# Two-layer graph network: where the rows' attention sums of the front stage are computed, and which engine issues the stores of the turned edges

## The reference

```
# layer 0, 8 heads of 64
wh    = (x @ weight).reshape(n, 8, 64)
awh_i = (wh * linear_i).sum(axis=2)      # the rows' attention sums
awh_j = (wh * linear_j).sum(axis=2)
e     = leaky_relu(awh_i[:, None, :] + awh_j[None, :, :], 0.2)
a     = softmax(e + ((1 - adj) * -1e10)[:, :, None], axis=1)
x     = layernorm(x + einsum('ijh,jhf->ihf', a, wh))
# layer 1, 8 heads of 64
adj1  = maximum(adj, eye)
q, k, v = projections of x with Wqs, Wks, Wvs
s     = q @ k.T / 8 + 0.01 * eye - 1e16 * (1 - adj1)
x     = layernorm(x + einsum('hqm,hmk,hko->qo', softmax(s), v, Wo))
```

## Time and profile before

| what | value |
|---|---|
| median of three timed runs | 4205.13 us (4201.45 to 4205.21) |
| the profiled execution: its own time | 4191.47 us |
| its span, first to last instruction | 4189.7 us |
| PE busy | 3770.2 us (90%) |
| DVE busy | 3506.9 us (84%) |
| ACT busy | 3342.6 us (80%) |
| POOL busy | 429.4 us (10%) |
| mean granted TensorE clock | 0.962 |

### The profile page before, as it was taken

The page is one execution under the profiler, slowest core; times in us unless marked ns, Lnnn a source line. Parts: engine busy times, 40 slices in busy tenths (PEclk is TensorE's granted clock), DMA queues, the critical chain, the costliest instruction groups (busy, mean ns, idle before and its releaser), DMA issues. The chain is left out here.

```text
span 4189.7 us, 104540 instructions
## 1 busy us (share of the span) xinstructions
PE 3770.2 (90%) x42880; PEld 2512.5 (60%) x42880; DVE 3506.9 (84%) x6040; ACT 3342.6 (80%) x4233; POOL 429.4 (10%) x634
## 2 busy tenths in 40 slices
PE   7991499999999959959999999999999999999977
PEld 4551499999999924425555555555555555555533
DVE  6657799999999977678888888888888888888734
ACT  3434699999999822239999999999999999999932
POOL 1211000000000000010110201102111021120100
PEclk9995699999999979969999999999999999999989
DMA  9999855555555377773543534435344353453133
GB/s 339 392 307 229 257 185 167 181 188 189 184 192 166 122 206 241 217 188 92 137 119 90 151 90 130 113 98 152 96 123 128 91 141 100 112 138 92 39 113 140
DMA packets 364121, 674.35 MB, mean 161 GB/s; under 512 B 79584, under 2 KB 239408, under 8 KB 326784
## 3 DMA queue, kind: packets, MB, share of 16 engines
q1 hardware_dynamic: 296448, 574.83, 45.9%
q0 software_dynamic: 24064, 84.37, 6.6%
q10 hardware_dynamic: 43136, 8.53, 1.1%
HBM read 524.43 MB, written 143.20 MB: 159 GB/s over the span
## 5 line engine op out<-in xcount | busy, mean ns | idle before, releaser
L1241 DVE CUSTOM_DVE_ANT_0 m_junk<-m_rough,m_rows 128x1024 bf16<-128x1024 f32 x1006 | 1230.8, 1223 | 220.6 <-PE m_rough L1109 207.6
L1187 ACT ACTIVATE m_scores<-m_strip 128x1024 f32<-128x1024 fp8e4 x1024 | 1052.4, 1028 | 121.5 <-DVE m_most L1241 56.8
L1201 ACT ACTIVATE m_whole<-m_scores 128x1024 int32<-128x1024 f32 x1024 | 1037.9, 1014 | 15.8 <-PE m_scores L1142 5.5
L632 PE MATMUL g_acc<-g_vals,g_pos 128*128 128x130 f16 x8192 | 956.6, 218 | 49.3 <-DVE g_neg L587 49.3
L549 ACT ACTIVATE g_step<-g_arow,k_steep 128x512 fp8e4<-128x512 f32 x1536 | 948.4, 707 | 40.7 <-DVE g_pos L580 37.7
L632 PE MATMUL g_acc<-g_vals,g_neg 128*128 128x130 f16 x8192 | 956.1, 221 | 0.0
L1123 PE MATMUL m_acc<-m_v,m_halves 128*128 128x129 f16 (+1 forms) x16384 | 896.8, 208 | 45.4 <-ACT m_got L1164 45.4
L1123 PEld LDWEIGHTS m_acc<-m_v,m_halves 128*128 128x128 f16 x16384 | 750.8, 98 | 280.1 <-issue 185.8
L632 PEld LDWEIGHTS g_acc<-g_vals,g_pos 128*128 128x128 fp8e4 x8192 | 802.1, 98 | 60.2 <-DVE g_neg L587 36.5
L1137 PE MATMUL m_scores<-m_qA,m_kA 128*128 128x512 f16 x2048 | 780.7, 381 | 10.0 <-ACT m_scores L1187 5.4
L632 PEld LDWEIGHTS g_acc<-g_vals,g_neg 128*128 128x128 fp8e4 x8192 | 785.0, 96 | 0.0
(11 more groups left out here) (162 smaller groups left out, 3034.6 us busy)
## 6 DMA issues: line engine op xcount, KB each, us to landing
g_vals<-scr_gat_v SPq DMA_DIRECT2D x128, 1040.0 KB, 5.1
m_v<-scr_v SPq DMA_DIRECT2D x64, 1032.0 KB, 7.7
a_stage<-in_adj SPq DMA_DIRECT2D x64, 1024.0 KB, 9.4
m_kA<-scr_k_hi SPq DMA_DIRECT2D x128, 512.0 KB, 6.2
scr_row_mask<-a_rowm SPq DMA_DIRECT2D x64, 512.0 KB, 8.0
m_rows<-scr_row_mask POOLq DMA_DIRECT2D x64, 512.0 KB, 7.0
m_kB<-scr_k_lo SPq DMA_DIRECT2D x64, 512.0 KB, 5.3
scr_gat_v<-a_early POOLq DMA_DIRECT2D x32, 520.0 KB, 10.6
```

The lines of the kernel that those rows point to most:

```text
L632: mm = pe.matmul(acc[:, b, it, lo:hi], edges[:, n % RING, t, rows], vals[:, b, 4 * j + t, lo:hi], start=j == 0 and t == 0 and lo == 0, sto ...
L1187: nc.scalar.activation(scores[:, n % 2], strip[:, 2 * st:2 * st + 2, :].rearrange("p t i -> p (t i)"), ACT.Copy, bias=-BIG, scale=BIG / ED ...
L1201: nc.scalar.activation(whole[:, st % 2], scores[:, st % 2], ACT.Exp, scale=0.125).then_inc(exped, 1)
L1241: nc.vector.tensor_tensor_reduce(out=junk[:, n % 2], in0=rough_of(m), in1=rows[:, n % TC, n // TC * WIDE:(n // TC + 1) * WIDE], scale=1.0, ...
```

## The change

PE's `project` no longer computes `ps_a`. A new `turn_back(c)` transposes the four 16 x 128 pieces of `aT` into `ps_a`, after the turns of the next chunk, for the last chunk ahead of the sum on `k.ones`. ACT copies the 64 columns at once in a new `copy_a(c)`. `ps_wh` now waits for the copy of two tiles before. DVE waits for `a_copied` before it copies `aij`, and for `a_done` before it overwrites `aT`. The stores of `colm` go from SP to ACT, each directly behind the copy of the second half, after a wait for that copy; the final waits for them go to ACT too. The copy of the last chunk's sums stands on ACT between the flips of groups 49 and 50.

```
@@ sync
-            def store_col(g):
-                sp.wait_ge(copied, 2 * g + 2)
-                gate(sp, passed)
-                sp.dma_start(col_v[:, g % C * TC:(g % C + 1) * TC, g // C, :], colm[:, g % 2]).then_inc(col_out[g % 2], 16)
...
-                if g > 0:
-                    store_col(g - 1)
-            store_col(G - 1)
...
-                sp.wait_ge(col_out[b], 16 * G // 2)
@@ tensor
-                if n > 0:
-                    pe.wait_ge(wh_copied, 2 * n)
+                if n >= 2:
+                    pe.wait_ge(wh_copied, n - 1)
                 for kb in range(KB):
-                    pe.matmul(ps_wh[:, n % 2, :], xT[:, c % 2, kb, t * P:(t + 1) * P], w[:, kb, :], start=kb == 0, stop=kb == KB - 1)
-                for kb in range(KB):
-                    mm = pe.matmul(ps_a[:, 0:2 * H], xT[:, c % 2, kb, t * P:(t + 1) * P], w2[:, kb, :], start=kb == 0, stop=kb == KB - 1)
+                    mm = pe.matmul(ps_wh[:, n % 2, :], xT[:, c % 2, kb, t * P:(t + 1) * P], w[:, kb, :], start=kb == 0, stop=kb == KB - 1)
                 mm.then_inc(wh_done, 1)
+
+            def turn_back(c):
+                pe.wait_ge(aT_copied, c + 1)
+                if c > 0:
+                    pe.wait_ge(a_copied, c)
+                for t in range(TC):
+                    mm = pe.transpose(ps_a[:, t * 2 * H:(t + 1) * 2 * H], aT[:, c % 2, t * P:(t + 1) * P], k.identf[0:2 * H, 0:2 * H])
+                mm.then_inc(a_done, 1)
...
+                if c > 0:
+                    turn_back(c - 1)
                 for t in range(TC):
                     project(TC * c + t)
...
-            pe.wait_ge(wh_copied, 2 * NT)
+            turn_back(C - 1)
+            pe.wait_ge(wh_copied, NT)
@@ vector
-                dve.wait_ge(wh_copied, 2 * n + 1)
+                dve.wait_ge(wh_copied, n + 1)
...
                     dve.wait_ge(a_out[c % 2], 16 * (c // 2))
+                    dve.wait_ge(a_done, c - 1)
...
-            dve.wait_ge(wh_copied, 2 * NT)
+            dve.wait_ge(a_copied, C)
@@ scalar, copy_flipped
+                if half == 1:
+                    act.wait_ge(copied, n + 1)
+                    act.dma_start(col_v[:, g % C * TC:(g % C + 1) * TC, g // C, :].bitcast(F16), colm[:, g % 2].bitcast(F16)).then_inc(col_out[g % 2], 16)
@@ scalar
                 nc.scalar.copy(wh[:, n, :], ps_wh[:, n % 2, :]).then_inc(wh_copied, 1)
-                nc.scalar.copy(aij[:, n, :], ps_a[:, 0:2 * H]).then_inc(wh_copied, 1)
+
+            def copy_a(c):
+                act.wait_ge(a_done, c + 1)
+                nc.scalar.copy(aij[:, c * TC:(c + 1) * TC, :], ps_a[:, 0:TC * 2 * H].rearrange("p (t a) -> p t a", t=TC)).then_inc(a_copied, 1)
...
+                if c > 0:
+                    copy_a(c - 1)
...
-            for n in range(2 * EACH * C, 2 * (EACH * C + 2 * AHEAD)):
+            for n in range(2 * EACH * C, 2 * (EACH * C + AHEAD)):
+                copy_flipped(n)
+            copy_a(C - 1)
+            for n in range(2 * (EACH * C + AHEAD), 2 * (EACH * C + 2 * AHEAD)):
                 copy_flipped(n)
...
+            for b in range(2):
+                act.wait_ge(col_out[b], 16 * G // 2)
@@ attend
-                    gate(pool, passed_p)
+                    gate(pool, passed)
...
-                gate(dve, passed_v)
+                gate(dve, passed)
```

More of the change, by code:

```diff
@@ L172, in front @@
         t_done, t_copied, wh_done, wh_copied = (s.sem(n) for n in ("t_done", "t_copied", "wh_done", "wh_copied"))
+        a_done, a_copied = s.sem("a_done"), s.sem("a_copied")
         aT_done, aT_copied, sum_done, topped = (s.sem(n) for n in ("aT_done", "aT_copied", "sum_done", "topped"))
@@ L956, in attend @@
         copied, got_used, chain, o_ready = s.sem("copied"), s.sem("got_used"), s.sem("chain"), s.sem("o_ready")
-        o_out, passed, passed_p, passed_v = (s.sem(n) for n in ("o_out", "passed", "passed_p", "passed_v"))
+        o_out, passed = s.sem("o_out"), s.sem("passed")
         block = ctx.enter_context(nc.Block())
@@ L1311, in finish @@
         chain, var_ready, rooted, normed = s.sem("chain"), s.sem("var_ready"), s.sem("rooted"), s.sem("normed")
-        z_out, passed, passed_v = [s.sem("z_out0"), s.sem("z_out1")], s.sem("passed"), s.sem("passed_v")
+        z_out, passed = [s.sem("z_out0"), s.sem("z_out1")], s.sem("passed")
         block = ctx.enter_context(nc.Block())
```

## The result

| | median us | runs | lowest to highest |
|---|---|---|---|
| before | 4204.06 | 6 | 4198.45 to 4205.21 |
| after | 4187.76 | 6 | 4183.20 to 4190.89 |

The ratio is 0.9959, with a 95% interval of 0.9949 to 0.9970: the change saves 16.3 us. The forecast was a saving of 8.1 us, so the sign was right and the size half of what was measured.

The account below looks back on a forecast made before the run. PE was taken to pace the chunk loop by a hair over the DMA engines, the table loop to be near DMA-bound with holes from the late store. -1.5 + 1.4 - 8 = -8.1 us off 4205.1 gave 4197, range 4180 to 4212.

Parts of the forecast that it names:

- The table loop: Table loop: the earlier store ends ACT's long waits and fills DMA holes, -8 us (bounds -16 and +6).
- The front is a sum of absolute times, so I take it off the median: Whole kernel: the front's -8.1 us, summed from the profile, was taken off the timed median of 4205.1 us, giving 4197.
- the forecast case: Whole kernel: the summed terms hold, -3 to -16 us, alone 4189 to 4202 us; chance 0.50.
- rival 1: Chunk loop: DMA engines have more to give; 4187 us at 410 GB/s, 4173 if they follow PE; chance 0.20.
- The chunk loop: Chunk loop: PE's path shortens but the DMA engines allow little of it, -1.5 us (bounds 0 and -25.9).
- a dip would show nothing: Chunk loop: a short stretch at PE's lower clock would show nothing, as PE gains 3 us a chunk to hide it.
- the sign that I had named: Chunk loop: if the forecast is right, PE now waits for `a_edge`, with chunks still 30.3 to 30.7 us apart.
- best 10 us: Chunk loop: the highest DMA rate found over 10 us was 395 GB/s, so a chunk takes 30.6 us.
- The bridge: Bridge: four transposes (0.4 us) and two store issues (0.5 each) lengthen the path, +1.4 us (0 to 2.6).
- rival 3: Table loop: ACT is held issuing stores, twelve issues at 1 us, no hole filled; 4218 us, slower; chance 0.12.
- Rival 2: Table loop: the store lands no earlier where it counts, loop gives -1 us, total 4204, no change; chance 0.18.
- Later stages: Stages after the front: merged counters are incremented as often and waited on by nobody, so nothing changes.

Follow-up runs that it names:

- after_light: The changed kernel with only a quarter of each adjacency group loaded for groups 3 to 47; 4164.76 us in one execution.
- counters_only: The kernel before with only the merged counters of attend and finish; 4204.80 us, ratio 1.0002.
- sp_early: The kernel before, stores still on SP, but from group 52 on issued ahead of the wait for the next group's mask; 4183.01 us, ratio 0.9950.
- act_late: stores_only with each store from group 51 on issued by ACT only when it begins the next group's copy; 4189.80 us, ratio 0.9968.
- sums_only: The changed kernel with the stores of the turned edges back on SP at their old place; 4207.69 us, ratio 1.0003.
- stores_only: The kernel before with only the stores of the turned edges moved to ACT's queue; 4188.79 us, ratio 0.9961.
- after_again: The changed kernel, unaltered, run again on the same chip as the separate parts; 4188.02 us, ratio 0.9962.
- spread_after: The changed kernel with groups 50 and 51 flipped first and the column sum spread, three tiles before each later group's flips; 4169.39 us, ratio 0.9919.
- before_look: A second profiled execution of the kernel before, nothing changed; 4206.03 us.

## Why the prediction was right, and where its size was off

**The table loop** was the right place, the mechanism was right, and its term of -8 us was mis-sized. The wait of 13.66 us and its kin are gone; the share is 1.05 to 1.07 in every window of 324 to 444 us; ACT waits for `scr_gat_v` in its place, as forecast. From the exponential to the next stage the loop went from 156.8 to 148.0 us against the profile that I read, 8.8 us, which is the term. Against the second execution of before it went from 167.9 to 148.0, 19.9 us, and to 150.6, 17.3 us, in the second of after. The step that failed is "The front is a sum of absolute times, so I take it off the median": the profiled execution stood 0.3% below the median, and I took the difference for something that lies beside the change. It lay in the very holes that the change fills. It could have been asked for: the own time was 10 us below the lowest of the timed runs, and of waits of the same kind, three groups apart, one was 13.7 us and the others 10.0 and 5.7. The lower bound of that term, -16, was also too tight for this reason.

That the range held is in part luck. The measured 4187.8 lies below what the forecast case gives by itself (4189 to 4202) and almost on the number of rival 1 (4187). Only because the range left room for rival 1 did it take the result in, and the traces, not the time, tell the two apart.

**The chunk loop** went as forecast in its cause, and by more than its term. PE's path is 3.4 us shorter per chunk (`after_light`), the middle chunks are still 30.4 to 32.3 us apart at 390 GB/s, and rival 1, engines with more to give, is refuted. The loop still ended 5.3 us earlier, not 1.5. The first chunk, in which PE waits for nothing in either kernel from 36 us to the reduction, gives 2.7 us (the first reduction at 56.7 in place of 59.4), and the last 2.5 (28.2 in place of 30.7). The last has no loads of x beside it: its 11.03 MB in 28.2 us are 391 GB/s, the same rate with less to move. The second chunk gives 1.7 us that are not the change's: in before the granted clock was 0.95 there and a projection call took 5.40 us in place of 3.70 (the chunk 32.4 us), in after it was 1.00. The five chunks between lose 1.5. Three kernels with the old sums, `counters_only`, `sp_early` and `act_late`, had no such dip, and their loops end at 273.7 to 274.7 us; against these the lead of after is 3.0 to 4.0. The forecast that a dip would show nothing after the change held in the chunk from 212 to 242 us, which took 30.35 us at a clock of 0.89.

PE's matmuls stood for `a_edge` only 3.0 us between 34 and 271 us, and 13.6 for ACT's copies, which wait for their stores; PE's weight loads, which go ahead of the matmuls, stood 16.9 us for `a_edge`. So the sign that I had named is half there. The waits that show the new bound are DVE's: in 90 to 240 us, first before, then after,

```profile
DVE a_rowm L321 <- DMA scr_row_mask<-a_rowm: 5.3, 7, 1.3
...
DVE a_edge L318 <- DMA a_stage<-in_adj: 0.6, 2, 0.4
```

```profile
DVE a_edge L319 <- DMA a_stage<-in_adj: 24.0, 23, 3.0
DVE a_rowm L322 <- DMA scr_row_mask<-a_rowm: 22.0, 27, 3.2
```

The prediction's "best 10 us" of 395 GB/s was not the best; in before,

```profile
156.70:166.70 10.00, 8.00 (x47) 4.69 (x44) 7.06 (x9) 4.42 (x6) 5.33 (x4) 1.00 1.07 401
```

A chunk at 401 would take 30.1 us, and the term would have been -4.8 us and not -0.8. What a chunk needs is the rate over 30 us, and there 395 was right: in no profile did the loop come above 397 GB/s over 20 us, or 394 over 50. The ceiling of 435 GB/s that the Trainium skill gives (DMA: Bandwidth & Descriptors, Specifications) would have made the loop 23 us shorter; this traffic did not show it.

**The bridge** was put at +1.4 us and took +6.0 (40.84 against 34.86); in the second execution of after +3.1 (37.94). Its two issues cost what was said: from the end of the sum to the exponential 5.3 us against 4.1. The rest I had at 0.4. But ACT now waits 2.97 and 2.95 us for its stores before two of its copies and PE 3.17 us for ACT, and the sum starts 6.1 us behind the last reduction, not 3.1. It is tempting to call this a backlog that the full loop hands over. `after_light`, whose loop runs at a share of 0.85, has the same wait, and its sum starts 5.5 us behind the last reduction:

```profile
251.47 1.93 ACT L424 CAST a_colm<-a_flipped 128x1024 fp8e4<-128x1024 bf16 x2 [3.15 <-DMA scr_edge_T<-a_colm]
```

So does `sums_only`, with its stores on SP (5.8 us), while `stores_only` keeps the 3.1. The wait comes with the turned-back sums; why is not shown. The sum then takes 29.4 us and not 27.7: the granted clock is 0.87 in 277 to 290 us, where it was 1.00 in the sum before. That is not constant: in `after_again` it is 1.00 and the sum takes 27.7 us. DVE's wait for `a_copied` came to 8.5 us and was covered, as forecast. So chunk loop and bridge together gave +0.65 us in this execution (311.50 against 310.85), where -0.1 was summed: right, by two errors that cancel. In `after_again` the exponential came at 307.2, which is -3.6.

**ACT held in the issue** (rival 3) is refuted: ACT's issues of these stores take 0.37 us as a rule and none over 0.45 in the seven profiles that have them, and 0.44 us shows behind each copy that ACT waits for itself. Long issues stayed with SP, on its loads: 6.3 us at most in after, 9.8 in `spread_after`. **Rival 2**, a store that lands no earlier where it counts, fell with the 17 to 20 us that the table loop lost.

Of the two rules on queues, the Trainium skill's sentence that issuing from several engines saves only the sequencer's time (DMA: Bandwidth & Descriptors, Issuing engines are not separate DMA queues) fits the chunk loop, where the stores landed after 7.3 us on SP and 7.3 to 7.7 on ACT, and is too strict for the table loop: there, in one queue with the loads, they landed after 17.9 and 20.0 us in `before_look` and `sp_early`, in a queue of their own after 14.5 and 15.0 in after and `act_late`. That agrees with its account of engines that take their queues in turn (same page, Queues, rings and completion order), but no run shows the turn itself. In the table loop both ways come to the same length, as shown above.

**Later stages** were put at nothing, and here 4 us were missed. The attention stage is 2219.3 to 2221.5 us in all six profiles of kernels with turned-back sums, and 2214.4 to 2217.1 in all eight without. `counters_only` (2216.7) excludes the counters. In `sums_only` the bridge (39.6) and the table loop (169.6) had already used up the 6 us by which its chunk loop was ahead, and in its profile the attention stage added some 5 us. It is also part of why `after` is no faster than `stores_only`. From `stores_only` to after all of it arises in the first 70 us of the stage, and some 3 us can be located. At the start of the stage ACT stores an offset of 1 KB and issues the load of it when it has landed; first `stores_only`, then after:

```profile
1819.82 0.34 ACTq L1164 DMA_DIRECT2D scr_offset<-m_offset  x1
1830.80 0.49 ACTq L1168 DMA_DIRECT2D m_qB<-scr_offset  x1
```

```profile
1822.31 0.34 ACTq L1183 DMA_DIRECT2D scr_offset<-m_offset  x1
1836.03 0.49 ACTq L1187 DMA_DIRECT2D m_qB<-scr_offset  x1
```

The landing takes 9.7 to 11.0 us in the eight profiles without turned-back sums and 12.9 to 14.4 us in the six with them, under the same loads on SP's queue, and PE waits for it (4.9 us in `stores_only`, 6.1 in after). The transfers move more slowly meanwhile (237 against 251 GB/s). Why, in code that the change does not touch, stays open; no run here changed anything of that stage by itself.

The accounts close with this. Second execution of before to after, as profiled: next stage 479.4 to 459.5, -19.8; attention +3.5; the other stages +1.3; span 4203.9 to 4188.9, -15.1 (parts rounded). Measured as medians: -16.3.

## What to carry to other kernels

Before a forecast is made against one profiled execution, compare its own time with the timed runs: if it lies outside them, the difference has a place in the trace, and a loop whose waits depend on when transfers land is the first place to look. Repeated waits of one kind that differ in length are the sign, and the longest of them may be the usual one. Time saved ahead of a serial piece of work (here the column sum) may show only when that piece is taken off the path as well: moving the sum into a stretch where PE was idle gave 18.4 us on top of the change, which itself gave 16.3.

## What the runs showed of the hardware

- In the table loop stores of 256 KB landed later in SP's queue, with its loads of 1 MB, than in ACT's queue: medians of 17.9 and 20.0 us (`before_look`, `sp_early`) against 15.0 and 14.5 (`act_late`, after). The store of group 52 in `before_look` was issued at 333.05 us, 0.1 us behind the end of a load's issue, and landed 23.0 us later. In the chunk loop, at a share of 1.07, the queue made no such difference (7.3 us on SP, 7.3 to 7.7 on ACT).
- Single issues held SP for 7.7 to 9.8 us in the table loop of nine of the 14 profiles (9.56 us in before), for a load or for a store of 256 KB; the same stores on ACT's queue never took above 0.45 us to issue. What holds SP is not shown.
- In this mix of loads and stores the DMA engines gave 394 GB/s at most over 50 us, and 401 to 403 over the best 10, at a share of 1.07; with a quarter of the loads of adj PE alone set the pace.
- A stage whose code is unchanged can change by 4 us in 2217 when another stage's instructions change, and keep that through all variants.
